# Moving the gated layer's first tile into the first stage's planned order of steps

## The reference

```python
x = x + _layernorm(_L0_attn_ref(_layernorm(x), ...))   # stage A
x = x + _layernorm(_L0_ffn_ref(_layernorm(x), ...))    # stage B
x = x + _layernorm(_L1_attn_ref(_layernorm(x), ...))   # stage C
x = x + _layernorm(_L1_ffn_ref(_layernorm(x), ...))    # stage D

def _qlora_linear(x, wq, A, B):                        # a gated layer's linear map
    w = jnp.tile(wq, (1, 4))
    return x @ w.T + x @ A.T @ B.T * 0.5
def _L0_ffn_ref(x, w1q, a1, b1, w3q, a3, b3, w2q, a2, b2):
    gate = jax.nn.silu(_qlora_linear(x, w1q, a1, b1))
    up = _qlora_linear(x, w3q, a3, b3)
    return _qlora_linear(gate * up, w2q, a2, b2)
```

## Time and profile before

| | |
|---|---|
| median of three runs | 2481.34 us |
| the profiled execution | 2484.96 us |
| its span | 2483.2 us |
| PE busy, share of the span | 2176.5 us, 88% |
| DVE / ACT / POOL busy | 1392.5 / 919.7 / 974.2 us |
| granted PE clock, mean | 0.932 |
| stage A | 0 to about 425 us |
| stage B | about 425 to about 885 us |

### The profile page before, as it was taken

How to read it: one execution, slowest core, us unless ns; L and a number is a source line. 1 busy time by engine, 2 the same in 40 slices (tenths; PEclk the granted TensorE clock), 3 DMA queues, 4 the chain that set the end, 5 groups by cost and what they waited for, 6 DMA issues and landing times.

```text
span 2483.2 us, 30799 instructions
## 1 busy us (share of the span) xinstructions
PE 2176.5 (88%) x11008; PEld 1538.1 (62%) x11008; DVE 1392.5 (56%) x3136; ACT 919.7 (37%) x1623; POOL 974.2 (39%) x751
## 2 busy tenths in 40 slices
PE   4899973899999969789899889898887499999998
PEld 4655532788888858655555455555543287667676
DVE  7855764677677742375555555555563056553333
ACT  5644553333233322125454454454445122221111
POOL 1333553644444410016665556566656422110000
PEclk9999986899999979889999899999987699999999
DMA  5310256112122146422224522222222355334232
GB/s 162 101 59 1 72 176 218 62 69 76 68 82 81 60 147 239 101 49 53 57 70 113 162 57 74 73 67 61 54 64 64 125 196 170 130 119 169 110 111 94
DMA packets 139573, 249.27 MB, mean 100 GB/s; under 512 B 26890, under 2 KB 69770, under 8 KB 139196
## 3 DMA queue, kind: packets, MB, share of 16 engines
q1 hardware_dynamic: 130716, 230.51, 29.3%
q10 hardware_dynamic: 8704, 16.78, 2.1%
HBM read 139.48 MB, written 76.02 MB: 87 GB/s over the span
## 4 chain that ended last, share of the span: by engine, by line
PE 55%; POOL 16%; issue 5%; DVE 5%; DMA 3%; ACT 3%; SPq 2%; POOLq 0%; ACTq 0%; DVEq 0%
POOL c_S L2081 13%; PE PS L2264 4%; PE PS L2221 4%; PE PS L2222 4%; PE PS L2225 4%; PE PS L1024 3%; PE PS L1732 3%; PE PS L1025 3%; PE PS L1026 3%; PE PS L1716 3%; PE PS L1747 3%; PE PS L1057 2%; PE PS L1058 2%; PE PS L1059 2%; PE PS L1692 2%
## 5 line engine op out<-in xcount | busy, mean ns | idle before, releaser
L1881 ACT ACTIVATE c_P<-PS 128x512 f32<-128x512 f32 (+3 forms) x768 | 356.2, 493 | 386.6 <-PE PS L1732 341.0
L2081 POOL TENSOR_TENSOR c_S<-c_S,c_P 128x2048 f32<-128x2048 f32 (+1 forms) x96 | 337.2, 3512 | 12.9 <-ACT c_P L1881 6.7
L1716 PE MATMUL PS<-c_K,c_Q 96*128 96x512 f32 (+3 forms) x768 | 282.8, 379 | 52.5 <-DVE cst L1998 31.2
L1732 PE MATMUL PS<-c_Q,c_K 97*128 97x512 f32 (+3 forms) x768 | 295.8, 398 | 10.7 <-ACT c_P L1881 6.1
L1732 PEld LDWEIGHTS PS<-c_Q,c_K 97*128 97x128 f32 x768 | 155.3, 204 | 186.3 <-issue 83.4
L1994 DVE TENSOR_REDUCE cst<-PS 128x1 f32<-128x512 f32 x256 | 176.3, 689 | 136.5 <-PE PS L1716 136.2
L2064 POOL TENSOR_SCALAR_AFFINE_SELECT c_P<-c_P 128x512 f32<-128x512 f32 x128 | 85.3, 667 | 356.3 <-ACT c_P L1881 356.3
L1716 PEld LDWEIGHTS PS<-c_K,c_Q 96*128 96x128 f32 x768 | 157.9, 206 | 100.0 <-DVE cst L1998 49.9
L1747 PE MATMUL PS<-c_P,c_V 128*32 128x512 f32 (+3 forms) x1536 | 183.0, 551 | 38.5 <-POOL c_P L2064 26.6
L1998 DVE CUSTOM_DVE_ANT_0 PS<-PS,maskw 128x128 f32<-128x128 f32 (+3 forms) x256 | 126.9, 510 | 124.1 <-PE PS L1716 123.6
L199 POOL TENSOR_TENSOR maskw<-maskw,mhalf 128x1 f32<-128x1 f32 x64 | 36.8, 574 | 357.9 <-DVE maskw L168 357.9
...
## 6 DMA issues: line engine op xcount, KB each, us to landing
...
c_Q<-c_qh SPq DMA_DIRECT2D x256, 64.0 KB, 2.0
...
```

The costliest lines, as they stand in the source:

```text
L1716: e.matmul(bank[:, 0:hi - lo], self.Q4[0:96, 4 * (o % 3) + g, 128 * t:128 * t + 128], self.K4[0:96, HEADS[o % 8], lo:hi], start=True, stop ...
L1732: e.matmul(self.k.bank(i % 3)[:, 0:hi - lo], self.K4[0:97, HEADS[o % 8], 128 * kt:128 * kt + 128], self.Q4[0:97, 4 * (o % 3) + g, lo:hi], ...
L1881: e.activation(self.P[:, R % 3, g, 0:hi - lo], self.k.bank(i % 3)[:, 0:hi - lo], ACT.Exp, scale=SCALE).then_inc(self.exp_s.s, 1)
L2081: e.tensor_tensor(S[:, :, 512 - n:512], before[:, :, 512 - n:512], P[:, :, 0:n], ADD).then_inc(self.psum_s.s, 1)
```

## The change

1. **The plan holds the whole first tile of stage B**: its transposes, low-rank products, sum, split, six `up`, `silu`, `gate`, `acc`, `gf`, and the transposes and low-rank products of tile 1. Stage B's own loops start at tile 1.
2. **Rests on POOL**: the rests of `w13` chunks 0 to 2 (six) are on POOL, those of 3 to 5 stay on DVE. Of the six rests of `w2` three go to DVE.
3. **Loads**: `bx` and `a2` are issued by ACT, after `affine 3,8` and after the stores of tiles 6 and 7 have landed; `xn` of tile 0, `a13`, `sel` by SP behind tile 8; `w2` is one transfer, issued by SP behind tile 13's stores, and its six casts stand in the plan.
4. **PSUM pairs**: `out` of tiles 12 to 15 takes the pairs 2, 0, 1, 3. Before an `out` may write, the `y` that read the pair's last content is done: for tile 12 that is `y` of tile 11 now; it was tile 9. The transposes of stage B wait for tile 12's `y` in place of tile 14's.
5. **Memory**: `xin`, `hid3`, `w2h`, `gfh` and `gfl` have other places. The input rows' places lie over `w2h`'s last two slices, so the last two casts wait for two more stores.

```diff
     def out_pair(t):
-        return t % (t // 4 + 1) if t >= 8 else t % 2 if t >= 4 else 0
+        return (2, 0, 1, 3)[t - 12] if t >= 12 else t % 3 if t >= 8 else t % 2 if t >= 4 else 0
...
-        add("in", 8.0, ("nextb", 0), ("xn_", 11), ("affine", 3, 8))
+        layers = "affine", 3, 8
+        add("act", .5, ("b_ld", 0), ("xn_", 7), layers)
         for c in range(6):
...
+                add("pool" if c < 3 else "dve", 2.35 if c < 3 else 1.15, ("b_wlo", i), ("b_whi", c),
+                    ("b_wlo", i - 1) if i not in (0, 6) else None)
...
+        add("in", 10.0, ("b_ld2", 0), ("xn_", 12))
+        for i in range(6):
+            add("act", 1.15, ("b_w2hi", i), ("b_ld2", 0), ("y", 15), ("xn_", 13) if i > 3 else None, ("b_w2hi", i - 1) if i else None)
+            add("pool" if i < 3 else "dve", 2.4 if i < 3 else 1.25, ("b_w2lo", i), ("b_w2hi", i))
...
+        for c in range(6):
+            add("pe", 3.0, ("b_up", c), ("b_xlo", 0), ("b_lowd", 0), ("b_blo", 0), ("b_wlo", 2 * c + 1), ("b_wlo", 5),
+                ("b_up", c - 1) if c else None, ("b_gate", c - 2) if c > 1 else ("y", 13 + c))
...
-            if t == 11:
+            if t == 8:
                 e.wait_ge(*self.affine(self.nth["affine", 3, 8]))
-                for u in (6, 7):
-                    e.wait_ge(*k.sty[u % 2](T.stores(u)))
-                self.then.sp_first(e)
-            if t == 14:
+                e.wait_ge(*k.sty[0](T.stores(0)))
+                self.then.sp_first(e)
+            if t == 12:
                 self.then.sp_xn(e, 1)
+            if t == 13:
+                e.wait_ge(*self.omm(NT))
+                for u in (10, 11):
+                    e.wait_ge(*k.sty[u % 2](T.stores(u)))
+                self.then.sp_w2(e)
+            if t == 14:
+                self.then.sp_xn(e, 2)
...
+    def sp_w2(self, e):
+        e.dma_start(self.w2[0:115, :, :], self.k.io["w2x"].rearrange("(c p) n -> p c n", p=115)).then_inc(self.ld2.s, 16)
...
+    def act_ld(self, e):
+        k, T = self.k, self.first.tail
+        for t in (6, 7):
+            e.wait_ge(*k.sty[t % 2](T.stores(t)))
+        e.dma_start(self.bx_in[:, :], k.io["bx"]).then_inc(self.ldb.s, 16)
+        e.dma_start(self.a2[:, :], k.io["a2"].partition_broadcast(128)).then_inc(self.lda.s, 16)
```

More of the change, by code:

```diff
@@ new lines, in plan @@
+        add("in", 12.0, ("b_ldb", 0), ("b_ld", 0))
+        add("act", 2.6, ("b_bhi", 0), ("b_ldb", 0))
+        add("dve", 3.1, ("b_blo", 0), ("b_bhi", 0))
+        add("in", 10.0, ("b_ld2", 0), ("xn_", 12))
+        for i in range(6):
+            add("act", 1.15, ("b_w2hi", i), ("b_ld2", 0), ("y", 15), ("xn_", 13) if i > 3 else None, ("b_w2hi", i - 1) if i else None)
+            add("pool" if i < 3 else "dve", 2.4 if i < 3 else 1.25, ("b_w2lo", i), ("b_w2hi", i))
+        for t in range(2):
+            add("in", 3.0, ("b_ldn", t), ("b_tr", 1) if t else ("xn_", 8), layers)
+            for u in (2 * t, 2 * t + 1):
+                add("pe", .5, ("b_tr", u), ("b_ldn", t), ("b_xt", u - 1) if u % 2 else ("b_lowd", 0) if t else ("y", 12))
+                add("act", .65, ("b_xt", u), ("b_tr", u), *((("b_fold", 0), ("b_xsum", 0)) if u == 2 else ()))
+            add("pe", .9, ("b_fold", t), ("b_xt", 2 * t + 1))
+            add("act", .3, ("b_usb", t), ("b_fold", t), ("b_low", 0) if t else None)
+            add("pool", 2.1, ("b_xsum", t), ("b_xt", 2 * t + 1), ("b_xlo", 0) if t else None)
+            add("act", .45, ("b_xhi", t), ("b_xsum", t))
+            add("dve", .45, ("b_xlo", t), ("b_xhi", t))
+            add("pe", .3, ("b_low", t), ("b_usb", t))
+            add("act", .8, ("b_lowc", t), ("b_low", t))
+            add("dve", .45, ("b_lowd", t), ("b_lowc", t))
@@ L1060, in pe_down, with first_pe @@
         m.then_inc(self.down_s.s, 1)
-    def pe(self, e):
-        for hf in range(2):
-            self.pe_trans(e, 0, hf)
-        self.pe_fold(e, 0)
-        self.pe_low(e, 0)
-        for t in range(NT):
+    def first_pe(self, e, name, i):
+        if name == "b_tr":
+            self.pe_trans(e, i // 2, i % 2)
+        elif name == "b_fold":
+            self.pe_fold(e, i)
+        elif name == "b_low":
+            self.pe_low(e, i)
+        else:
+            self.pe_up(e, 0, i)
+    def pe(self, e):
+        for t in range(1, NT):
             for c in range(6):
                 self.pe_up(e, t, c)
-                if t > 0 and c in (0, 2):
+                if c in (0, 2):
                     self.pe_gtr(e, t - 1, c // 2)
@@ L1096, in act_w2hi @@
     def act_w2hi(self, e, i):
-        e.wait_ge(*self.ld2[i // 3](1))
+        e.wait_ge(*self.ld2(1))
+        if i > 3:
+            T = self.first.tail
+            for t in (12, 13):
+                e.wait_ge(*self.k.stx[t % 4](T.places(t)))
         e.copy(self.w2h[0:115, i, :], self.w2[0:115, i, :]).then_inc(self.w2hi_s.s, 1)
@@ L1143, in act_ghi, with first_act @@
                ).then_inc(self.ghi_s.s, 1)
+    def act_ld(self, e):
[4 more added lines that the diff above has]
+        e.dma_start(self.a2[:, :], k.io["a2"].partition_broadcast(128)).then_inc(self.lda.s, 16)
+    def first_act(self, e, name, i):
+        if name == "b_ld":
+            self.act_ld(e)
+        elif name == "b_whi":
+            self.act_whi(e, i)
+        elif name == "b_bhi":
+            self.act_bhi(e)
+        elif name == "b_w2hi":
+            self.act_w2hi(e, i)
+        elif name == "b_xt":
+            self.act_xt(e, i // 2, i % 2)
+        elif name == "b_usb":
+            self.act_usb(e, i)
+        elif name == "b_xhi":
+            self.act_xhi(e, i)
+        elif name == "b_lowc":
+            self.act_low(e, i)
+        else:
+            self.act_silu(e, 0, i)
     def act(self, e):
         T, y = self.tail, self.k.bank(6, 2)
-        for hf in range(2):
-            self.act_xt(e, 0, hf)
-        self.act_usb(e, 0)
-        self.act_xhi(e, 0)
-        self.act_low(e, 0)
-        for t in range(NT):
+        for t in range(1, NT):
             for c in range(6):
                 self.act_silu(e, t, c)
-                if t == 1 and c < 3:
-                    for i in range(2 * c, 2 * c + 2):
-                        self.act_w2hi(e, i)
-                if t > 0 and c in (0, 2):
+                if c in (0, 2):
                     self.act_ghi(e, t - 1, c // 2)
@@ L1234, in dve_glo, with first_dve @@
                         self.gfh[0:115, cs, :].bitcast(F32), SUB).then_inc(self.glo_s.s, 1)
+    def first_dve(self, e, name, i):
+        if name == "b_wlo":
+            self.wlo(e, i).then_inc(self.wlod_s.s, 1)
+        elif name == "b_blo":
+            self.dve_blo(e)
+        elif name == "b_w2lo":
+            self.w2lo(e, i)
+        elif name == "b_xlo":
+            self.dve_xlo(e, i)
+        elif name == "b_lowd":
+            self.dve_low(e, i)
+        elif name == "b_gate":
+            self.dve_gate(e, 0, i)
+        elif name == "b_acc":
+            self.dve_acc(e, 0, i)
+        else:
+            self.dve_u2(e, 0)
     def dve(self, e):
@@ L1238, in dve @@
         own = self.k.mine["dve"].on(e)
-        self.dve_xlo(e, 0)
-        self.dve_low(e, 0)
-        for t in range(NT):
+        for t in range(1, NT):
             for c in range(6):
-                if t > 0 and c == 5:
+                if c == 5:
                     e.wait_ge(*self.down_s(2 * t))
@@ L1306, in pool_gf, with first_pool @@
         e.tensor_tensor(self.gf[:, c, 0:m], self.g2[:, 0:m], self.g2[:, m:2 * m], ADD).then_inc(self.gf_s.s, 1)
+    def first_pool(self, e, name, i):
+        if name == "b_wlo":
+            self.wlo(e, i).then_inc(self.wlop_s.s, 1)
+        elif name == "b_w2lo":
+            self.w2lo(e, i)
+        elif name == "b_xsum":
+            self.pool_xsum(e, i)
+        else:
+            self.pool_gf(e, 0, i)
     def pool(self, e):
         T = self.tail
-        self.pool_xsum(e, 0)
-        for t in range(NT):
+        for t in range(1, NT):
             for c in range(6):
-                if t > 0 and c == 5:
+                if c == 5:
                     T.pool_y(e, t - 1)
@@ L1319, in pool @@
                     T.pool_x(e, t - 2)
-                if t == 1 and c < 3:
-                    for i in range(2 * c, 2 * c + 2):
-                        self.pool_wlo(e, i)
         T.pool_x(e, 14)
```

91 lines of the change are left out of this document (46 added, 45 removed).

## The result

Over 20 runs each, the changed kernel takes a median of 2492.32 us (2485.63 to 2502.08), the kernel before 2483.16 us (2478.11 to 2487.18): a ratio of 1.0038, 95% interval 1.0028 to 1.0049, so 7 to 12 us slower. Forecast were 2471 us and a range of 2455 to 2484; the prediction was wrong, in sign too. The profiled execution took 2489.69 us (span 2487.9, mean clock 0.930).

A forecast was written before the change was run, and what follows sets the result against it. Stage B, PE alone from 484 us, was taken as the bound, its end set by tile 2's low-rank copy. 483.3 - 473.0 = 10.3 us takes 2484.96 to 2474.7; with that execution 3.6 above the median, 2471, range 2455 to 2484.

The forecast's parts named there:

- D: Time from R to the low-rank copy of tile 2; 123.7 us before, the forecast amounts to 113.3.
- gain of 10.3: Low-rank copy of tile 2 in stage B forecast at 473.0 in place of 483.3, so 10.3 us gained.
- R: When `affine 3,8` can start, at the end of DVE's scaling ahead of it; 359.7 in before's first profile.
- the copy: Stage B's copy of tile 2's low-rank rows, at 483.34 before; forecast at 473.0.
- nearer to the lone one: Tile 8's store beside ACT's two loads: taken as 8 us, between 6.1 alone and 14.8 behind `bx` and `a2`.
- first rival: `w2` is there in time, landing at 430, and DVE is the bound: 23 us gained, 2458; chance 0.18.
- the pace of a tile at full clock: Stage B, from release of tile 1's `up` c = 2 to the low-rank copy: 14.7 us, as a PE-bound tile takes.
- The order of the layers' steps shifts by a place here and there; I take 0, between 4 us lost and 4 gained.: Stage A's layer steps, listed under edits with no price: 0 us, 4 each way.
- nothing else in the change can: Stage B: only moving tile 2's low-rank copy at 483.34 moves the kernel's end, by as much.
- The third: POOL's rests hold up DVE in stage A's last blocks: 6.8 us net, 3.5 gained, 2478; chance 0.17.
- The fourth: Stores of tiles 8 and 9 get no turn beside ACT's loads: `y` of tile 11 after about 392, 2487; chance 0.11.
- over 30 us: Sum if all removed waits around stage B's start, and tile 1's work moved beside stage A, came as gain.

The follow-up runs named there:

- a2_gap: Changed kernel with `a2` issued by ACT behind `y` of tile 11, no longer ahead of tile 8's store; 2483.70 us, ratio 1.0010 to the kernel before.

## Why the prediction was wrong

**How the miss divides.** The median was forecast at 2471 and came at 2492.3, 21 us higher. Over three profiles each, D is 11.5 us above what the forecast's gain of 10.3 would have left of before's, R is 3.9 us later and the part behind the copy 1.8 us longer. Another 1.8 us lie in the kernel before, whose median was 2483.16 over 20 runs and 2481.34 over the first three. The remaining 2 us are in no profile. So two steps failed, the chain in size and the order in sign.

**The step that failed for the size: the chain's gain of 10.3 us was not there.** D should have fallen from 123.7 to 113.3; it was 124.6. Step by step, in the profile whose R was that of before (forecast in brackets; a `gate` is given by its end, as in the forecast):
- Store of tile 8: taken as 8 us, "nearer to the lone one"; it took 12.7 (365.04 to 377.77), so `y` of tile 10 was 3.4 us late. `a2_gap` shows the cause: without `a2` beside it the store takes 6.4 us, and `y` of tile 10 is 7 us sooner. A second queue did not shield the store.
- `y` of tile 11 at 383.5 (381.5 to 382.7), the statistics of tile 12 at 389.5 (387.4): these steps held, 2 us late.
- `xn_` of tile 12 ended at 408.6 (404): the rest of `bx` took 4.88 us in place of 3.05. POOL's addition ran beside it from 394.23 to 396.58; that this stretched it is likely, not shown.
- The first `silu` came at 422.6 (418.6), `w2` was issued at 425.2 (422) and there at 451.3 (447): 26.1 us for 25. Right in size. `gate` of c = 4 at 454.4 (450.4).
- `gate` of c = 5 at 460.6 (454.3), the first of tile 1 at 467.2 (458.3). DVE's three rests of `w2` took 7.6 us (3.22, 2.75 and 1.59) and stand ahead of these gates: the `silu` had ended at 457.2 and 460.6, and their gates began 2.8 and 5.9 us later, when DVE was free. The forecast's chain has no term for these rests, only its first rival has. The `silu` of tile 1:

```profile
460.07 0.55 ACT L1183 ACTIVATE b_g<-PS 128x460 f32<-128x460 f32 x1
```

- From there to the copy 16.7 us, not 14.7. The forecast took the pace of a tile at full clock. Here PE was at the lower level for 3.4 us. Its products came 0.38 us apart there and 0.21 apart at full clock, which is 1.5 of the 2.0 us:

```profile
468.00:471.40 3.40, 3.40 (x11) 2.96 (x10) 3.25 (x9) 0.00 (x0) 2.19 (x3) 0.53 0.00 1
```

**The step that failed for the sign: "The order of the layers' steps shifts by a place here and there; I take 0, between 4 us lost and 4 gained."** D was within 1.2 us of before's, so most of what lifts the median lies elsewhere: 3.9 us in R, 1.8 behind the copy, 2 in no profile. 107 of PE's 228 steps stand elsewhere, not one here and there. Laid down in the kernel before, the new order cost 13 us (9 to 17). In the changed kernel, R was on average 3.9 us later over its three profiles (364.7 against 360.8), and in eight of twelve with that order PE had twice the time at the lower clock between 150 and 250 us. I had looked at the places that the chain touched, and not at the 250 us ahead of them. But the long stretches are not the whole cause: with the old order laid down for the first 285 us they were gone, and the ratio stayed at 1.0040. What in the order costs the time stays open.

**The sentence "nothing else in the change can".** The forecast let only the copy of tile 2 move the end. The pace of 28.5 us a tile held, as it had asked, but the part behind the copy varied by 6.7 us among three executions of the changed kernel.

**The rivals.** The first (`w2` in time, 23 us gained) did not happen, and its price was too high: with a fast load D was 8.6 us below before (9.5 below the changed kernel), since that load still took 16.8 us and not 8. The third was wrong; its sum is off too (6 x 2.3 less 6 x 1.1 is 7.2, not 6.8), which changes nothing. The fourth was half right: `y` of tile 11 at 383.5, not after 392, but the stores did suffer from ACT's loads. The "over 30 us" that I set out from were not all fiction: with three waits shortened D is 19.2 us below the changed kernel's and 18.3 below before's, and the median 12 us below before.

**What stays open.** The three profiles of the changed kernel exceed the three of before by 6.9 us on average (3.9 in R, 1.2 in D, 1.8 behind it), the medians by 9. The part behind the copy took 1997.3 to 2004.0 us with the changed kernel and 1999.1 to 1999.8 with before. It goes roughly with the time that PE spent there at the lower clock, by the trace's clock records: 224.3 us in the execution of 1997.3, 239.5 in that of 2002.5, 241.3 in that of 2004.0, and over all twenty profiles from 197.2 (1996.7) to 249.3 (2004.8). Why one order of the layers meets the lower clock twice as long as another was not found, only that it does so in most of its executions.
